# A graph network's gathers on one core: the last pass of each sum split in two, and the first sources loaded apart

## The reference

```
def _rgcn_layer(x, W, SW, b, src, dst, rel):
    xt = jnp.einsum('nd,rde->rne', x, W)
    msg = xt[rel, src]
    agg = jax.ops.segment_sum(msg, dst, num_segments=x.shape[0])
    return jax.nn.relu(agg + x @ SW + b)
...
feat = jax.nn.relu(x @ W1 + b1)
h = feat * d_invsqrt
agg = jax.ops.segment_sum(h[src], dst, num_segments=N)
feat = feat - agg * d_invsqrt
return feat @ W2 + b2
```

## Time and profile before

| | us |
|---|---|
| median of 3 runs (range) | 6351.35 (6350.53 to 6352.94) |
| the profiled execution: its own time | 6353.09 |
| its span, first to last instruction | 6351.3 |
| POOL busy | 4719.5 (74% of the span) |
| PE busy | 3434.3 (54%) |
| DVE busy | 1586.1 (25%) |
| ACT busy | 507.8 (8%) |

### The profile page before, as it was taken

The page is one execution under the profiler, slowest core; times in us unless marked ns, Lnnn a source line. Parts: engine busy times, 40 slices in busy tenths (PEclk is TensorE's granted clock), DMA queues, the critical chain, the costliest instruction groups (busy, mean ns, idle before and its releaser), DMA issues. The chain is left out here.

```text
span 6351.3 us, 51898 instructions
## 1 busy us (share of the span) xinstructions
PE 3434.3 (54%) x13350; PEld 2426.7 (38%) x13500; DVE 1586.1 (25%) x2504; ACT 507.8 (8%) x1112; POOL 4719.5 (74%) x4994
## 2 busy tenths in 40 slices
PE   4565556556565756566556656653444434344443
PEld 2333333333343534333333333333333334333333
DVE  4333433433343112122221212211111111111111
ACT  1000000000010101011110111110000000000000
POOL 6777777777777677777777777757777777777776
PEclk7776777767777767677667777765555555555555
DMA  3222222222222122222222222222222222222221
GB/s 74 59 59 59 59 56 59 59 59 59 59 59 59 52 64 74 61 69 69 69 69 61 77 61 69 69 60 58 63 61 64 62 57 68 58 62 62 62 63 55
DMA packets 207369, 396.37 MB, mean 62 GB/s; under 512 B 87746, under 2 KB 96756, under 8 KB 207332
## 3 DMA queue, kind: packets, MB, share of 16 engines
q0 software_dynamic: 159456, 326.88, 19.7%
q1 hardware_dynamic: 47876, 69.05, 3.4%
HBM read 363.49 MB, written 32.10 MB: 62 GB/s over the span
## 5 line engine op out<-in xcount | busy, mean ns | idle before, releaser
L538 POOL DMA_INDIRECT r_rows<-h_d,r_idx x1661 | 1568.8, 944 | 542.1 <-issue 505.9
L538 POOL DMA_INDIRECT r_rows<-x_d,r_idx x1661 | 1576.0, 949 | 531.5 <-issue 505.8
L538 POOL DMA_INDIRECT r_rows<-in_x_dram,r_idx x1661 | 1571.8, 946 | 533.7 <-issue 505.8
L681 PE MATMUL bank<-r_S,r_rows 128*128 128x128 f32 x6644 | 1218.9, 356 | 987.4 <-DMA r_rows<-in_x_dram,r_idx 455.9
L681 PEld LDWEIGHTS bank<-r_S,r_rows 128*128 128x128 f32 x6644 | 1135.5, 263 | 967.1 <-issue 957.2
L845 PE MATMUL bank<-r_S,r_rows 128*128 128x64 f32 x3322 | 768.4, 424 | 1111.2 <-DMA r_rows<-h_d,r_idx 1099.1
L845 PEld LDWEIGHTS bank<-r_S,r_rows 128*128 128x128 f32 x3322 | 726.4, 330 | 1155.7 <-DMA r_rows<-h_d,r_idx 621.2
L720 DVE TENSOR_TENSOR r_S<-bank,key 128x1792 f32<-128x1792 f32 x238 | 480.1, 2017 | 996.4 <-PE bank L681 993.7
L628 ACT COPY r_agg<-bank 128x512 f32<-128x512 f32 x476 | 279.1, 586 | 2558.2 <-PE bank L681 2558.2
L689 PE MATMUL bank<-r_agg,w1s 128*128 128x512 f32 (+1 forms) x480 | 446.7, 1099 | 24.1 <-ACT r_agg L628 24.1
L689 PE MATMUL bank<-r_agg,w2s 128*128 128x512 f32 (+1 forms) x480 | 446.3, 1098 | 24.1 <-ACT r_agg L628 24.1
(11 more groups left out here) (142 smaller groups left out, 1300.8 us busy)
## 6 DMA issues: line engine op xcount, KB each, us to landing
r_rows<-in_x_dram,r_idx POOLq DMA_INDIRECT x1661, 2.5
r_rows<-x_d,r_idx POOLq DMA_INDIRECT x1661, 2.5
r_rows<-h_d,r_idx POOLq DMA_INDIRECT x1661, 2.5
d_xr<-in_x_dram SPq DMA_DIRECT2D x48, 256.0 KB, 2.7
x_d<-d_yr SPq DMA_DIRECT2D x24, 256.0 KB, 2.1
d_x1r<-x_d SPq DMA_DIRECT2D x24, 256.0 KB, 2.7
z_d<-d_zr SPq DMA_DIRECT2D x24, 256.0 KB, 2.3
feat_d<-d_fr SPq DMA_DIRECT2D x24, 256.0 KB, 2.1
```

The source lines that it names most:

```text
L538: pool.indirect_dma_start(out=self.rows[:, s, :], out_offset=None, in_=self.table[:, :], in_offset=bass.IndirectOffsetOnAxis(ap=self.idx[: ...
L681: mm = pe.matmul(agg_ps[j][:, bass.ds(offs[j * KG + k], TK)], g.rows[:, h * KG + k, :], S[:, pb, j * KG + k, :], start=False, stop=(k == t ...
```

## The change

It has two parts.

The end of each sum: LEFT becomes two parts, pair 0 (14 tiles), and pairs 1 and 2 (23 tiles). In by_chunk chunk 23's tail stands between the two and chunk 24's behind the second. In LEFT the mixing and the adds go pair by pair (16 records over 128 columns each) rather than once. For the last pair PE waits for each group's tiles in two halves, on semaphores of their own. SP stores chunk 23's tables before chunk 24's. rounds_i gets a further condition: one more round if a group of the second part begins below node 12,288.

The prologue: SP first issues a small load of the first 56 tiles' sources, which DVE casts, PE turns and ACT copies straight into r_idx. Relations are loaded by ACT's queue. The way through DRAM falls away: PE spreads tlo over 128 partitions and thi to one by 14 matmuls each against the identity, and DVE copies or reduces them from PSUM. The place of several copies changes between ACT and DVE. off_i is laid out by pairs in 16 columns and is cleared once.

```diff
+
+class Part:
+
+
+    def __init__(self, at, tiles):
+        self.at, self.tiles, self.groups = at, tiles, len(tiles)
+        self.pairs = range(at, at + len(tiles) // PAIR)
+
+    def of(self, h):
+        return self.tiles[h - self.at * PAIR]
+
+
+FULL = Part(0, [KG] * RING)
+LEFT = Part(0, [min(KG, TILES - g * KG) for g in range(IT * RING, NG)])
+LEFT_PARTS = [Part(0, LEFT.tiles[:PAIR]), Part(1, LEFT.tiles[PAIR:])]
+ENDS = len(LEFT.pairs)
 NGP = NG // PAIR
...
+    def sync(self, sync):
+        sync.dma_start(self.early_i[:, :], self.edges[self.SRC][0:UN * P].rearrange("(p e) -> p e", e=P)
+                       ).then_inc(self.early_in, 16)
         sync.wait_ge(self.padded, 3)
...
-        sync.wait_ge(self.tiles, 2)
-        for to, of in ((self.tile_lo_d, self.tlo), (self.tile_hi_d, self.thi)):
-            sync.dma_start(to.rearrange("(j p) -> p j", p=TB), of[:, :], allow_slow_non_contiguous=True
-                           ).then_inc(self.tile_out, 16)
-        sync.wait_ge(self.tile_out, 32)
-        sync.dma_start(self.c.lo_b[:, :], self.tile_lo_d.partition_broadcast(P)).then_inc(self.lo_in, 16)
-        for to, of in ((self.glo7, self.tile_lo_d), (self.ghi7, self.tile_hi_d)):
-            sync.dma_start(to[:, :, :], of.rearrange("(p g k) -> p g k", g=2, k=KG)).then_inc(self.group_in, 16)
+        self.load_edges(sync, self.DST)
+        self.load_edges(sync, self.SRC)
...
+        pe.wait_ge(self.ident_done, 1)
+        pe.wait_ge(self.early_cast, 1)
+        pe.transpose(c.psum[self.EARLY_BANK][:, 0:UN], self.early_f[:, :], c.ident[0:UN, 0:UN]
+                     ).then_inc(self.early_turned, 1)
+
...
+        def bounds(of, parts, half, m):
+
+            bank, n = self.bank(m, half)
+            for j in range(n):
+                mm = pe.matmul(bank[0:parts, j * TB:(j + 1) * TB],
+                               of[:, 4 * m + j:4 * m + j + 1].broadcast_to([TB, parts]), c.ident[0:TB, 0:TB],
...
+        pe.wait_ge(idx_ready, PR)
+        for m in banks:
+            bounds(self.tlo, P, 1, m)
+        pe.wait_ge(self.tiles, 2)
+        for m in banks:
+            pe.wait_ge(self.node_out, m + 1)
+            bounds(self.thi, 1, 0, m)
...
+
+    def act(self, act, g):
         c = self.c
-        act.wait_ge(self.raw_in[1], 48)
-        act.copy(self.rawf[1], self.raw[1]).then_inc(self.other_f, 1)
-        act.wait_ge(self.raw_in[2], 48)
-        act.copy(self.rawf[2], self.raw[2]).then_inc(self.other_f, 1)
+        act.wait_ge(self.early_turned, 1)
+        act.copy(g.idx[:, :], c.psum[self.EARLY_BANK][:, 0:UN]).then_inc(g.idx_ready, PR)
+        act.wait_ge(self.padded, 3)
+        self.load_edges(act, self.REL)
         for m in range(self.BANKS):
-            act.wait_ge(self.turned, self.BANKS + m + 1)
-            self.place(act.copy, c.src_i, 1, m).then_inc(self.src_placed, 1)
...
+        act.copy(self.rawf[self.REL], self.raw[self.REL]).then_inc(self.rel_f, 1)
+        act.wait_ge(self.raw_in[self.SRC], 48)
+        act.copy(self.rawf[self.SRC], self.raw[self.SRC]).then_inc(self.src_f, 1)
...
+        for m in range(self.BANKS):
+            dve.wait_ge(self.turned, self.BANKS + m + 1)
+            self.place(dve.tensor_copy, c.lo_b, 1, m).then_inc(self.lo_out, 1)
+        dve.wait_ge(self.lo_out, self.BANKS)
         ch.then(dve.tensor_reduce(c.glo[:, :], by_group(c.lo_b), AX.X, ALU.min))
...
+        for m in range(self.BANKS):
+            dve.wait_ge(self.turned, 2 * self.BANKS + m + 1)
+            bank, n = self.bank(m, 0)
+            assert n * TB % KG == 0
+            to = self.ghi[:, 4 * m * TB // KG:(4 * m + n) * TB // KG]
+            dve.tensor_reduce(to, bank[0:1, 0:n * TB].rearrange("o (g k) -> o g k", k=KG), AX.X, ALU.max
+                              ).then_inc(self.hi_out, 1)
...
+        for at, part in enumerate(LEFT_PARTS):
+            first = IT * RING + part.at * PAIR
+            ch.then(dve.tensor_reduce(sp[:, 6 + at:7 + at], c.glo[0:1, first:first + part.groups], AX.X, ALU.min))
+            ch.then(dve.tensor_scalar(sp[:, 6 + at:7 + at], sp[:, 6 + at:7 + at], float((NCH - 2 + at) * CH), None,
+                                      ALU.is_lt))
+        ch.then(dve.tensor_tensor(sp[:, 6:7], sp[:, 6:7], sp[:, 7:8], ALU.max))
...
-    iteration(IT, LEFT)
-    late(eng, two, [])
+    for part, chunk in zip(LEFT_PARTS, two):
+        iteration(IT, part)
+        late(eng, [chunk], [])
...
+def halves(part, h):
+
+
+    tiles = part.of(h)
+    return (tiles + 1) // 2 if part is not FULL and h >= (ENDS - 1) * PAIR else tiles
...
+                    for k in range(part.of(h)):
+                        s, slot = h * KG + k, h if k < halves(part, h) else RING + h % PAIR
                         pool.indirect_dma_start(
...
+                        ).then_inc(self.landed[slot], 16)
...
+    def wait_rows(self, pe, part, h, i, k):
+
+        tiles, half = part.of(h), halves(part, h)
+        if k == 0:
+            pe.wait_ge(self.landed[h], (i * KG + half) * 16)
+        elif k == half:
+            pe.wait_ge(self.landed[RING + h % PAIR], (tiles - half) * 16)
...
-    NIT = IT + 1
...
+
+                def mix(at, h0, groups):
+                    pe.wait_ge(agg_out, n + (h0 + groups + BUFS))
+                    pe.wait_ge(added, q * NIT + i + (at + 1))
+                    for r in range(NREL):
+                        mm = pe.matmul(mix_ps[:, 0:groups * GN], W[:, r, :], agg[:, h0:h0 + groups, :, r],
+                                       start=(r == 0), stop=(r == NREL - 1))
+                    mm.then_inc(mixed, 1)
...
                     _, offs = nc.values_load_multi_w_load_instructions(
-                        c.off_i[0:1, bass.ds(i * RING + p * PAIR, PAIR), :], engines=bass.OrderedEngineSet([pe.engine]),
+                        c.off_i[0:1, bass.ds(i * PR + p, 1), :], engines=bass.OrderedEngineSet([pe.engine]),
...
+                    if part is not FULL:
+                        mix(p, p * PAIR, PAIR)
+                if part is FULL:
+                    mix(0, 0, RING)
...
-                    if tiles is FULL or p + BUFS < pairs:
+                    if ahead(part, p):
                         one_hot((p + BUFS) % PR, q, i + (p + BUFS) // PR, ch)
...
+                    if part is not FULL:
+                        add(p, starts[first:first + PAIR])
+                if part is FULL:
+                    add(0, load(c.gs_i, NPAD))
...
         settle(before)
-        store(*two)
+        for ch in two:
+            store(ch)
         settle(two[1], 2)
 
 
```

More of the change, by code:

```diff
@@ L165, with __init__ @@
 class Prologue:
[L171 removed]
+    def __init__(self, nc, ctx, c, edges, loads):
         def sb(name, shape, dt=F32):
@@ L530, in run, with iteration @@
     def run(self, pool, ready):
-        def iteration(q, i, tiles):
-            for p in range(len(tiles) // PAIR):
+        def iteration(q, i, part):
+            for p in part.pairs:
                 pool.wait_ge(self.idx_ready, (q * (IT + 1) + i) * PR + p + 1)
@@ L614, in _ @@
         if prologue:
-            prologue.act(act, g.first)
+            prologue.act(act, g)
         else:
@@ L621, in _, with iteration @@
         with act.Fori(0, rounds) as q:
-            def iteration(i, tiles):
+            def iteration(i, part):
                 n = act.snap(q * NG + i * RING)
@@ L625, in iteration @@
                 gate(act, c.passed)
-                for h in range(len(tiles)):
+                for h in range(part.at * PAIR, part.at * PAIR + part.groups):
                     act.wait_ge(summed, n + (h + 1 + RING))
@@ L629, in iteration @@
                              ).then_inc(agg_out, 1)
-                    if tiles is FULL and h % PAIR == PAIR - 1:
+                    if part is FULL and h % PAIR == PAIR - 1:
                         g.take(act, h // PAIR, q, i + 1)
@@ L724, in _, with ahead, part_steps @@
         first_steps = BUFS if counts else 0
-        def pass_steps(tiles):
-            pairs = len(tiles) // PAIR
-            ahead = pairs if tiles is FULL else max(pairs - BUFS, 0)
-            return (pairs + ahead if counts else 0) + len(tiles) - 1
-        round_steps = first_steps + IT * pass_steps(FULL) + pass_steps(LEFT)
+        def ahead(part, p):
+            return part is FULL or p + BUFS < ENDS
+        def part_steps(part):
+            adds = part.groups - 1 if part is FULL else len(part.pairs) * (PAIR - 1)
+            return (len(part.pairs) + sum(ahead(part, p) for p in part.pairs) if counts else 0) + adds
+        left_steps = [part_steps(part) for part in LEFT_PARTS]
+        round_steps = first_steps + IT * part_steps(FULL) + sum(left_steps)
         with dve.Fori(0, rounds) as q:
```

270 lines of the change are left out of this document (133 added, 137 removed).

## The result

The changed kernel takes 6295.66 us (median of 5 runs, 6293.33 to 6298.07) against 6351.53 (6350.53 to 6352.94): a ratio of 0.9912, 95% interval 0.9898 to 0.9925. The profiled execution took 6294.61 us for a span of 6292.8. (In three later series the median of the kernel before stands 10 to 14 us higher, and in the one that has the changed kernel again so does its own, 6309.22 against 6365.82; the ratio is 0.9912 there too.)

What follows compares the result with a forecast made beforehand. POOL's three runs of gathers, some 2,075 us each, and four stretches without gathers set the time. Gains of 24.6 + 6.9 + 7.2 + 7.5 = 46.2 us take the median from 6351.35 to 6305; range 6298 to 6314.

Steps and rivals of the forecast that it cites:

- The start: Prologue: POOL's first gather at 6.2 us instead of 31.80; gain 25.6 us, 24.6 net of 1.0 for slower gathers.
- The first rival: Start: early indices come, but a start nearer 12 us or slowed gathers cost 6 to 10 us: about 6313; chance 0.12.
- The fourth rival: First sum, second lap: POOL runs out of indices; slower than before once rounds_i comes after about 107 us; chance 0.01.
- the fifth: Round decision: the new condition adds a round, which costs three sums, over 6,200 us; chance 0.01.
- A pair's mixing: Relational sums' ends: 3.9 us for 128 columns; only the last pair's mixing and two adds stay on the path, 8.8 less.
- The third sum: Third sum's end: no mixing; shorter last tail (6.8 us) and 0.6 us from halved waits; gain 7.5 us (6 to 8.5).
- The first and second sum's ends: Adds and tails behind the last gathers: gains of 6.9 us (4.4 or 8.5) and 7.2 us (5.2 or 9.3).
- The clock, put between its levels: PE at both ends: shorter pieces with waits, so values between the 1.2 and 2.4 GHz results, 6.9 and 7.2 us.
- The rival with the low clock throughout: PE late at the ends: 4.4 and 5.2 us gained, 6309.5, or 6313 with two more us in each sum; chance 0.18.
- PE's return: PE back from chunk 23's tail at 2101.1 (1.2 us of it for registers) and, in the second sum, 4212.6.
- The tails for one chunk: Chunk 24's tail alone behind the adds: 1.4 us shorter in the first sum, 5.7 in the second.
- My third rival: Everything faster: start at 5.5 us, both ends at the high clock, mixing hidden; 6298 to 6301; chance 0.08.

Runs made afterwards that it cites:

- after_again: The changed kernel run once more without any change, on the chip of later runs; 6309.22 us against 6365.82 for the kernel before, ratio 0.9912.
- late30: The changed kernel with 18 added memsets of 1,666 columns on DVE in the prologue, some 30 us in all; ratio 0.9942 to the kernel before.
- no_halves: The changed kernel, but PE waits for all of a group's tiles also in pair 2, not for two halves; ratio 0.9914 to the kernel before.
- hot_later: The changed kernel, but in the relational sums pair 2's one-hots are built behind chunk 23's tail, not ahead of pair 0's adds; ratio 0.9912 to the kernel before.
- add_first: The changed kernel with DVE's adds of pair 0 ahead of its one-hots for pair 2; first and second sums' adds end 12.64 and 14.50 us behind the last gather.
- warm_second: hot_later with products of zeros, 10 and 18, in PE's two gaps of the second sum's chunk 23 tail; 6289.89 us, ratio 0.9906 to the kernel before.
- ends_only: The changed kernel's split last pass with the old prologue and its way through DRAM; ratio 0.9956 to the kernel before.
- tails_together: The changed kernel, but chunk 23's tail stands behind both parts, together with chunk 24's; ratio 0.993 to the kernel before.

## Why the prediction was right or wrong

**What bounds: right.** Three runs of gathers that nothing shortens, and four stretches without them; the table accounts for the span.

**The start: right, in part by luck.** 5.73 for 6.2 (6.59 in seven other traces). The small load let the cast run 1.4 us sooner than I had it, and ACT's table load of 1.28 us, which I had not counted, nearly made up for it. What came back is 1.4 us over the first 56 gathers, up to 2.8 in other traces, where I had 1.0 (0 to 3): that 1.0 also stands between the two whole sums is chance, since such sums differ by more between executions. Of the work new beside gathers the destinations' cast held one gather (1.42 us at 19.61, up to 1.87 elsewhere) and the reductions and small copies behind it next to none. The first rival, gathers that don't run freely, is refuted with it. rounds_i came at 50.53 for 46 because the destinations landed 7 us later than I had let them; with two queues loading at once the loads take longer. The cover I gave as 15 us is 13.1 (15.6 in after_again); late30's delay of 30 us went past it, and POOL waited. The fourth rival's mechanism is real and its condition wasn't met, and no round was added (1,661 gathers a sum, the fifth).

**A pair's mixing: nearly right.** 16 records over 128 columns took 3.96 us (3.9 forecast), and mixing by pairs, with the halves, brings 9.7 and 9.5 us (8.8).

**The third sum: right in sum** (7.4 for 7.5), with the tail saving 7.0 (19.34 to 12.36; 6.8 forecast) and the halves 0.4 (0.1 to 0.4 by no_halves) in place of 0.7.

**The first and second sum's ends: where it failed.** The forecast was 6.9 and 7.2; measured are 10.4 and 13.6. These 9.9 us are the miss: the medians fell by 55.9 where I had 46.2. (In the spans, 58.5, the shorter second run of gathers comes on top, and 0.5 at the start.) Three of its steps were off:

1. *The clock, put between its levels.* "The new end has the same work in shorter pieces with waits for copies between them; so I take values between the two levels." At least the upper end of each bound came, 8.5 and 9.3, 1.6 and 2.1 us more than I took. The clock is down through PE's wait for the tail, but behind it PE has 23 tiles and two mixings in store; it is back at 1.00 before pair 1's mixing, and the waits for copies between the pieces don't lower it here (1.00 in 2080 to 2090 and in 4180 to 4190). The rival with the low clock throughout (0.18) is refuted.
2. *PE's return.* "For loading its registers I estimate 1.2 more": in the traces PE zeroes at 2075.15, 0.1 us behind the four transposes (2073.90 + 1.13), and at 4172.96 right behind Tail2's last product (4171.68 + 1.49), so behind the transposes that term is nearly nothing (0.51 us in hot_later, where the transposes themselves ran at the high clock). Set against the last gather, PE is back 8.3 us ahead of it where I had 7.4, and 5.2 where I had 3.3 (Tail2 for one chunk was also 0.7 shorter). In the second sum the clock rose sooner behind it: the 14 tiles were done 4.7 us after the return (4172.96 to the end of its second group at 4177.7), where even my high bound had 6.0. In all the adds end 1.2 and 3.2 us below my high-clock bounds, which were 11.9 and 15.3 behind the last gather (2120.4 less 2108.49, 4231.2 less 4215.90). The second of these bounds holds a slip: "the same sum" as in the first, 23.4 or 19.3 us behind PE's return, would end at 4236.0 or 4231.9, and I had left out 0.7, the size of the adds. Without the slip the forecast for this end would have been 6.5, and its miss 0.7 larger. add_first shows that this return is what sets the end, at about one for one, and hot_later shows up to where it goes: to 9.5, the last landing. In warm_second PE is back 6.1 us ahead, 0.85 sooner than in the kernel after, its first seven tiles are 0.72 shorter, and the adds end 1.67 sooner: the return and the clock together.
3. *The tails for one chunk.* 2.1 and 6.8 us shorter where I had 1.4 and 5.7: 0.7 and 1.1.

Sums: 6.9 + 1.6 + 1.2 + 0.7 = 10.4, and 7.2 + 2.1 + 3.2 + 1.1 = 13.6. So the mechanism was right and these terms were mis-sized, all on one side. (With the second sum's adds of the other executions, 12.81 to 12.94, the 13.6 would be 12.8 to 12.9; the miss remains, and after_again's medians, 56.6 us apart, repeat it.) They were not independent: an earlier return and a higher clock come together in a PE that works off a backlog. My third rival named that case with 0.08, and even it, 6298 to 6301, stopped short, because it kept the 1.2 us and the tails' sizes.

**What stays open.** Whether warm_second is faster than the kernel after by the times: its pauses are 3.0 and 4.0 us shorter, 0.05%, and the ratios' intervals overlap. Why the clock falls and rises when it does: the 0.85 us by which the second sum's adds differ between two executions of after is the clock's, 0.45 in pair 1's first seven tiles (2.54 and 2.99 us) and 0.40 in PE's return, of which the first transposes, 0.80 and 1.13 us, make 0.33; but nothing in the program differs between the two, and in after_again the clock fell while the mixing ran. The low-clock case for a whole end wasn't made, so its price stays an estimate.

## What to carry to other kernels

When one queue sets the time and everything else hides beside it, measure each stretch in which it stands from the last thing it did; such distances repeated to within 0.9 us here between executions whose medians differ by 14 us. A tail put between two parts of the work costs the busy engine its hold time only until the last transfer has landed, so the end is the later of two things: the landing plus the last piece's work (9.5 us here), and the engine's return plus its backlog; reckon both. With a backlog behind its return PE was back at the high clock within the first 14 tiles in every trace here (in add_first's second sum it fell once more behind that), so for such an end start from the high clock rather than the middle, and look for the pause ahead of the backlog, where products of zeros can keep the clock; and an order of work moved within one block must be followed to the next instruction that stands behind it.

## What the hardware showed that I had not expected

- When ACT's and SP's queues loaded at once, ACT's load at L229 held its queue for 11.01 us and SP's of the sources at the same line for 14.05, where before, on SP's queue alone, such loads (L215) took 3.67 to 4.83; the destinations' cast moved from 11.67 to 19.11 (13.66 in ends_only, with the old loads).
- The granted clock can fall beside running products: in after_again at 2067.6, inside a mixing whose 16 records follow each other without a gap.
- The mixing's records don't follow the clock. In tails_together pair 1's mixing in the second sum took 4.09 us at a granted clock of 0.50 (below), and 3.96 at 1.00 elsewhere, while seven tiles of L761 fall from 3.36 to 1.72 us and the bf16 zeroing from 0.63 to 0.38. The mixing's operand agg[:, h, :, r] is read with a stride; whether that is the reason wasn't tried.

```profile
4174.00:4178.00 4.00, 4.00 (x17) 3.81 (x17) 0.08 (x1) 0.00 (x0) 3.08 (x4) 0.50 0.20 49
```

- POOL's gathers beside DVE's operations with two SBUF inputs were up to 2.50 us long, more than the 1.92 of before.
